# A fused attention and mixture-of-experts kernel: first four tiles prepared in pieces of 1, 1 and 2, side stages of attention in places of their own, local values moved by DMA

## The reference

```
x = layernorm(x + A(x))        # A: two attentions, each with a residual of its own
x = layernorm(x + F(x))        # F: a shared expert and 2 of 8 routed experts

A(x):  x = x + global_attn(rmsnorm(x, w1))     # causal over 1024, keys and values through a latent of 32
       x = x + local_attn(rmsnorm(x, w2))      # causal, window of 32
       both: 16 query heads, 4 key/value heads, 8 features each; rope, then each
       head of q and k divided by its rms; softmax(q k / sqrt(8)) v; output matrix wo
F(x):  shared = (silu(x sg) * (x su)) sd       # width 256
       p = sigmoid(x router + bias); the two largest, divided by their sum, weigh
       the outputs of their experts, each of width 256 like the shared one
```

## Time and profile before

| | us |
|---|---|
| median of 3 runs (lowest, highest) | 748.67 (747.52, 750.77) |
| profiled execution | 749.87 |
| its span, first to last instruction | 748.1 |
| busy PE, PEld, DVE, ACT, POOL | 639.4, 344.4, 505.7, 430.6, 379.6 |
| mean granted TensorE clock | 0.971 of full |
| moved by DMA | 47.23 MB |

### The profile page before, as it was taken

One profiled execution on the slowest core, in us unless ns is written; L12 is line 12 of the kernel. 1 busy time (PEld: TensorE's weight loads), 2 busy tenths in 40 slices (PEclk: granted clock), 3 DMA queues, 4 the chain that ended last, 5 costly groups with the idle time before them and its releaser, 6 DMA issues. The chain is left out here.

```text
span 748.1 us, 12565 instructions
## 1 busy us (share of the span) xinstructions
PE 639.4 (85%) x4147; PEld 344.4 (46%) x4147; DVE 505.7 (68%) x1325; ACT 430.6 (58%) x589; POOL 379.6 (51%) x420
## 2 busy tenths in 40 slices
PE   2378988998999999899999889999987999999950
PEld 1223332343453334454434344445765767666840
DVE  2568774467896458799559858658875658344864
ACT  4367876876566775567776644763442554344433
POOL 5366534554534434442153377751477256777831
PEclk9989998999999999999999999999999999999985
DMA  8235555200000000000000001010004122335251
GB/s 255 83 117 204 203 175 203 73 1 1 1 2 1 1 1 15 0 15 15 15 1 1 1 30 40 30 34 0 1 15 122 52 64 75 101 93 160 82 184 57
DMA packets 38126, 47.23 MB, mean 63 GB/s; under 512 B 8960, under 2 KB 35232, under 8 KB 37408
## 3 DMA queue, kind: packets, MB, share of 16 engines
q1 hardware_dynamic: 26976, 35.10, 15.2%
q0 software_dynamic: 4352, 9.05, 3.5%
q10 hardware_dynamic: 6736, 2.30, 1.2%
HBM read 35.29 MB, written 28.98 MB: 86 GB/s over the span
## 5 line engine op out<-in xcount | busy, mean ns | idle before, releaser
L878 ACT ACTIVATE prob<-ps_s 128x1024 f32<-128x1024 f32 x320 | 309.2, 1024 | 145.8 <-PE ps_s L1249 101.0
L1291 PE MATMUL ps_v<-prob,va 128*32 128x512 f32 x1152 | 155.8, 622 | 4.1 <-POOL prob L768 3.9
L1249 PE MATMUL ps_s<-qs,ks 32*128 32x512 f16 x576 | 102.1, 389 | 19.9 <-ACT prob L878 16.2
L768 POOL TENSOR_SCALAR_AFFINE_SELECT prob<-prob 128x1024 f32<-128x1024 f32 x64 | 70.5, 1120 | 42.8 <-ACT prob L878 42.5
L1033 DVE STREAM_TRANSPOSE sums<-ps_v 128x512 f32<-128x512 f32 x62 | 44.2, 714 | 68.1 <-PE ps_v L1291 35.1
L1529 POOL DMA_INDIRECT y_rows<-y,to_row x72 | 70.2, 975 | 38.7 <-DVE y L1650 21.1
L1249 PEld LDWEIGHTS ps_s<-qs,ks 32*128 32x128 f16 x576 | 25.3, 91 | 127.1 <-ACT prob L878 80.6
L1562 ACT ACTIVATE gated<-ps_gu 128x512 f32<-128x512 f32 x46 | 27.5, 597 | 79.3 <-PE ps_gu L1757 65.7
L1757 PE MATMUL ps_gu<-weights,rows_t 128*128 x144 | 68.2, 596 | 0.5 <-ACT rows_t L1567 0.5
L1285 PE MATMUL ps_v<-prob,vd 128*128 128x256 f32 (+1 forms) x292 | 59.1, 349 | 4.3 <-DVE marked L1053 3.9
L1138 PE MATMUL ps_p<-ident_half,zeros 128*128 128x512 f16 x216 | 52.8, 387 | 7.0 <-DVE k_rows L1024 2.5
(11 more groups left out here) (233 smaller groups left out, 1086.4 us busy)
## 6 DMA issues: line engine op xcount, KB each, us to landing
x_rows<-in_blank SPq DMA_DIRECT2D x8, 2112.0 KB, 8.8
rows<-x_rows SPq DMA_DIRECT2D x72, 66.0 KB, 2.0
chosen_y<-y_rows SPq DMA_DIRECT2D x8, 512.0 KB, 6.7
weights<-in_weights SPq DMA_DIRECT2D x1, 3456.0 KB, 13.7
out<-result ACTq DMA_DIRECT2D x8, 256.0 KB, 2.2
marked<-in_hidden SPq DMA_DIRECT2D x3, 512.0 KB, 5.4
r_in<-in_hidden SPq DMA_DIRECT2D x6, 256.0 KB, 2.7
y_rows<-y,to_row POOLq DMA_INDIRECT x72
```

Of the source, the lines that this page charges most:

```text
L768: pool.affine_select(out=probs_at(n, 0, SLOT_COLS), in_=probs_at(n, 0, SLOT_COLS), compare_op=ALU.is_ge, fill=0.0, base=0, pattern=[[0, SL ...
L878: act.activation(probs_at(n, 0, SLOT_COLS), scores_at(n, 0, SLOT_COLS), ACT.Exp, scale=HD ** -0.5 / GAIN ** 2).then_inc(exped, 1)
L1249: last = pe.matmul(scores_at(n, j * BANK, BANK).rearrange("p (r q) -> p r q", r=REP), ks[b % QUERY_BATCHES][rows, kt * P:(kt + 1) * P], qs ...
L1291: last = pe.matmul(bank[g * VW:(g + 1) * VW, :, :], va[b % VALUE_BATCHES][:, kt, g, :], probs_at(n + g // 2, g % 2 * BANK, BANK).rearrange ...
```

## The change

- `CHUNK_ORDER` begins with three small global chunks, (0,0,0) and (0,0,1) of one tile and (0,0,2) of two (`SMALL`), then (0,0,4) of four, so 18 chunks; chunks are now named by their first tile. All preparation stages work on `size_of(chunk)` tiles. The small ones use the table `PREPARE_SMALL` (11 steps), (0,0,4) `PREPARE_FIRST` (21 steps); local chunks have `PREPARE_LOCAL`.
- The first slot stands at step -29 and the first chunk starts at -40, the next at -37, -32, -27; two steps of pause stand before tile 1 and before tile 4, the pause ahead of the last local tiles has 40 steps instead of 38. By the planner's tables the first slot of tile 4 moves from step 20 to -5, and every later slot by 25 (after the pause 23); chunk (0,1,0) starts at -13 (before 0), the two next 13 and 14 steps earlier, (0,2,0) 16, and from (1,0,4) on all by 23 to 25.
- `turn_values`, `move_values` and the matrices `select` are gone. SP sends the value rows to `vd` itself, 16 transfers of 32 partitions x 4 x 32 bytes for each local chunk.
- Steps have three places: -0.5 (after scores on PE, after band on DVE), -0.25 (after wo, after add), 0 (after weighings, after sums). The tables have places in halves and quarters.
- SP's program follows the steps too.
- The zeroing of `kd` and `vd`, the ones and the band have other steps; the reciprocals of the sums are written into PSUM beside the sums instead of a buffer of their own.
- `WARM` has 155 products at 30 places instead of 221 at 30.
- In `expert_phase` the late tokens, turns, router, choice and `FINAL_SENDS` (8 to 10) come later by one to three pairs, and the last gather by one.

```diff
-FIRST_STARTS = (-37, -16)
-CLEAR_VALUES_AT, CLEAR_BLOCKS_AT = {-33: 1, -32: 2}, {-31: 0, -15: 1}
-ONES_AT, BLOCK_ONES_AT = {-20: 1, -18: 2}, {-6: 0, -4: 1}
-BAND_AT, REPEAT_BAND_AT = -36, -31
+FIRST_STEP = -29
+PAUSES = {(1, 3, 4): 40, (0, 0, 1): 2, (0, 0, 4): 2}
+SMALL = {(0, 0, 0): 1, (0, 0, 1): 1, (0, 0, 2): 2}
+FIRST_STARTS = (-40, -37, -32, -27)
+CLEAR_VALUES_AT = {-38: 1, -37: 2}
+CLEAR_KEYS_AT = {-22: 1, -28: 0}
+CLEAR_BLOCKS_AT = {-31: 0, -23: 1}
+ONES_AT = {-18: 2, -14: 1}
+BLOCK_ONES_AT = {-12: 0, 5: 1}
+BAND_AT = -8
+REPEAT_BAND_AT = -5
+PREPARE_SMALL = [(0, "square"), (1, "sum"), (1, "invert"), (1, "refine"), (2, "scale"), (3, "turn_tokens"), (3, "move_tokens"),
+                 (4, "project", 0), (4, "rotate", 0), (5, "add"), (5, "square_heads"), (6, "sum_heads"), (6, "invert_heads"),
+                 (7, "normalise"), (7, "split_heads"), (8, "pair_parts"), (9, "turn_parts", 2), (9, "move_parts", 2),
+                 (10, "turn_parts", 0), (10, "move_parts", 0)]
+PREPARE_FIRST = [(-0.25, 'square'), (1, 'sum'), (1, 'invert'), ..., (19, 'turn_parts', 2), (18, 'move_parts', 2), ..., (20, 'move_parts', 1)]
+PREPARE_LOCAL = [(0, 'square'), (3.5, 'sum'), ..., (15, 'rotate', 1), (16, 'add'), (16.75, 'send_values'), (16, 'square_heads'), ...]
+PLACES = (-0.5, -0.25, 0)
+START_DELAYS = {(1, 3, 4): 3, (0, 2, 4): 2, (1, 0, 0): -1, (1, 0, 4): 8, (1, 1, 4): -3, (0, 2, 0): -2, (1, 2, 4): -2}
+WARM = {('wo', 2): (3, 0), ('turn_parts', 3, 2): (3, 0), ('weigh', 9): (3, None), ('weigh', 37): (7, 0), ..., ('turn_parts', 2, 2): (9, 0)}
...
         def at_every_step(attend, stages):
             for s in STEPS_ALL:
-                attend(s)
-                for chunk, name, *where in beside.get(s, []):
-                    if name in stages:
-                        stages[name](chunk, chunk_number[chunk], *where)
+                for part, place in zip(attend, PLACES):
+                    part(s)
+                    for chunk, name, *where in beside.get(s + place, []):
+                        if name in stages:
+                            stages[name](chunk, chunk_number[chunk], *where)
...
+            def send_values(chunk, k):
+
+                _, b, c = chunk
+                sp.wait_ge(rope, rope_value(k, 1, "values"))
+                if b < 2:
+                    sp.wait_ge(cleared, GROUPS * (b + 1))
+                if b >= 2:
+                    sp.wait_ge(weighed, batch_weighed(1, b - 2))
+                blocks = vd[b % 2][:, c * P // KEYS:(c + CT) * P // KEYS, :].rearrange("p (t b) m -> p b t m", b=P // KEYS)
+                for of in range(P // KEYS):
+                    for g in range(GROUPS):
+                        sp.dma_start(blocks[g * KEYS:(g + 1) * KEYS, of, :, g * VW:g * VW + HD],
+                                     v_rows[of * KEYS:(of + 1) * KEYS, :, g * HD:(g + 1) * HD]).then_inc(values_out, 16)
...
+                inverse = sums_bank(q)[:, 0, 0:REP * P // VW].rearrange("p (r b) -> p r b", r=REP)
+                dve.reciprocal(inverse, sums[:, :, :, HD]).then_inc(inverses, 1)
...
-            def turn_values(chunk, k):
-
-                for b in range(4):
-                    last = pe.matmul(side_values(chunk)[:, b], select[:, b].rearrange("p g n -> p (g n)"), v_rows[:],
-                                     start=True, stop=True)
...
-LATE_TOKENS = {4: (0, 4), 5: (4, 8)}
-LATE_TURNS = (5, 6)
-LOGITS_AT, LATE_EXP_AT = 7, 9
-FINAL_SENDS = 8
+LATE_TOKENS = {4: (0, 2), 5: (2, 5), 6: (5, 8)}
+LATE_TURNS = (7, 9)
+LOGITS_AT = 10
+LATE_EXP_AT = 10
+FINAL_SENDS = 10
-GATHERED_AT = {0: 34, 1: 36, 3: 38, 2: 40, 6: 45, 4: 46, 7: 47, 5: 48}
+GATHERED_AT = {0: 34, 1: 36, 3: 38, 2: 40, 6: 45, 4: 46, 7: 47, 5: 49}
```

More of the change, by code:

```diff
@@ L4 @@
+import math
 from contextlib import ExitStack
@@ L78 @@
 ROW = D + 4
-SCAN, ENDS = 8, 8
+SCAN = 8
+ENDS = 8
 SHIFTS = tuple(tuple(2 ** n for n in range(6) if 2 ** n < tiles) for tiles in SHARE_TILES)
 END_SHIFTS = tuple(tuple(2 ** n for n in range(6) if 2 ** n < entries) for entries in LISTS)
-ROUTE = [(0, "route_add"), (1, "route_stats"), (2, "route_moments"), (4, "route_power"), (8, "route_token"), (10, "route_turn"), (12, "route_move"), (14, "route_logits"), (15, "route_bias")]
-CHOOSE = [(17, "choose_exp"), (18, "choose", "prob"), (20, "choose", "first"), (22, "choose", "second"),
-          (24, "choose", "third"), (26, "choose_rank"), (26, "choose", "weights"), (28, "choose", "totals"), (30, "choose", "scan"),
-          (32, "choose", "slots"), (34, "choose", "slot1"), (36, "choose", "slot2"), (42, "choose", "blocks"),
-          (46, "choose", "ends"), (50, "choose", "starts"), (54, "choose", "past"), (58, "choose", "rows"),
-          (62, "choose", "experts")]
@@ L95 @@
-ROUTE_AT = {0: 172, 1: 188, 2: 210, 3: 0, 4: 0, 5: 0}
+ROUTE = [(0.75, 'route_add'), (2.0, 'route_next'), (1, 'route_stats'), (2, 'route_moments'), (4, 'route_power'), (7.75, 'route_token'), (10, 'route_turn'), (10, 'route_move'), (15.5, 'route_logits'), (15, 'route_bias')]
+CHOOSE = [(17, 'choose_exp'), (18, 'choose', 'prob'), (20, 'choose', 'first'), (22, 'choose', 'second'), (24, 'choose', 'third'), (26, 'choose_rank'), (26, 'choose', 'weights'), (29, 'choose', 'totals'), (29, 'choose', 'scan'), (32, 'choose', 'slots'), (34, 'choose', 'slot1'), (36, 'choose', 'slot2'), (42, 'choose', 'blocks'), (46, 'choose', 'ends'), (50, 'choose', 'starts'), (54, 'choose', 'past'), (58, 'choose', 'rows'), (62, 'choose', 'experts')]
@@ new lines @@
+SENDS_FROM = 41
+SENT_INSIDE = 7
+SEND = [(SENDS_FROM + i * 3 // 2, "send", i) for i in range(2 * SHARE_TILES[0])]
+SECOND_INSIDE = [(17, 'choose_exp'), (17, 'choose', 'prob'), (18, 'choose', 'first'), (20, 'choose', 'second'), (20, 'choose', 'third'), (25, 'choose', 'weights'), (26, 'choose_rank'), (32, 'choose', 'totals'), (33, 'choose', 'scan'), (34, 'choose', 'slots'), (35, 'choose', 'slot1'), (36, 'choose', 'slot2')]
+INSIDE = [CHOOSE + SEND, SECOND_INSIDE + [(SECOND_INSIDE[-1][0] + 10 + i, "send", i) for i in range(SENT_INSIDE)]]
@@ L303, in slot_order @@
 def slot_order():
-    order, step, local = [], 0, iter((1, b, qt) for b in range(B) for qt in range(TPB))
+    order, step, local = [], FIRST_STEP, iter((1, b, qt) for b in range(B) for qt in range(TPB))
     banks = {}
@@ L405, in stages_beside @@
         for chunk, start in zip(CHUNK_ORDER, starts):
-            for when, *stage in PREPARE:
-                if stage[0] in ("turn_values", "move_values", "spread_keys") and not chunk[0]:
+            for when, *stage in table_of(chunk):
+                if stage[0] in ("send_values", "spread_keys") and not chunk[0]:
                     continue
@@ L426, in banks_of @@
                 moved = (SIDE_MOVES[stage[0]], *(("totals",) if stage[0] == "choose_rank" else stage[1:]))
-                free_from[bank] = start_of[chunk] + moved_at[k][moved] + 1
+                of_table = moved_at[k] if chunk[0] == 2 else {tuple(stage): when for when, *stage in table_of(chunk)}
+                free_from[bank] = start_of[chunk] + of_table[moved] + 1
                 bank_for[chunk, *stage] = bank
@@ L440, in attention_layers @@
     for chunk, start in zip(CHUNK_ORDER, starts):
-        needed = min(slot_step[n] for n, (q, _, _) in enumerate(slots) if tiles[q][:2] == chunk[:2] and tiles[q][2] // CT == chunk[2])
-        assert start + PREPARE_STEPS <= needed, (chunk, start, needed)
+        needed = min(slot_step[n] for n, (q, _, _) in enumerate(slots) if chunk_of[tiles[q]] == chunk)
+        assert start + max(when for when, *_ in table_of(chunk)) < needed, (chunk, start, needed)
     route_starts = []
     for k, (_, b, c) in enumerate(ROUTED):
-        start = max(ROUTE_AT[k], added_step[position[1, b, c * CT + CT - 1]] + 1)
+        start = max(ROUTE_AT[k], added_step[position[1, b, c + CT - 1]] + 1, route_starts[-1] + ROUTE_STEPS if k else 0)
         while banks_of(starts, route_starts + [start]) is None:
@@ L1228, in score @@
                 layer, b, qt = tiles[q]
[L1229 to L1231 removed]
+                chunk = chunk_of[tiles[q]]
+                if qt == chunk[2] and (kt == qt and pair == 0 or kt is None):
+                    pe.wait_ge(parts_out, turns_before(chunk_number[chunk] + 1))
                     if layer:
```

317 lines of the change are left out of this document (166 added, 151 removed).

## The result

The changed kernel takes **703.86 us** (median of 4 runs, 701.55 to 705.95) against 749.57 us for the kernel before in the same comparison: ratio 0.9392, 95% interval 0.9349 to 0.9436, 45.7 us faster. The forecast was 724 us, range 711 to 741: the direction was right, the size was off by 20 us.

A forecast was written before the change was run, and what follows sets the result against it. Neither PE nor ACT alone was taken to bound attention, but queues worked in a written order, with engines waiting for each other. 749.87 - 17.6 + 2 - 5 - 4 = 725.3 profiled, so 724 us; range 711 to 741.

The forecast's parts named there:

- Term C: Attention, 67 to 500 us: half and quarter places let side stages go ahead of a weighing; -4 us, -15 to +10.
- the rival in which side stages hold the queues up: Preparations and routings: stages placed half a step early make queues wait; gain gone or 753 us; chance 0.07.
- the places are worth what the idle time allows: Rival for the waiting in attention: Term C is -15 and Term A -20, so 711 us; chance 0.12.
- the mark: First score of tile 4, the 21st exponential: from 66.6 us before to 49.0 forecast, bounds 43.4 to 57.
- Term A: Start of the kernel: small first chunks bring attention earlier, -17.6 us (-23 to -9.6), with +2 for pushed-back steps.
- Both signs named for a wrong prediction: 21st exponential after 57 us; stretch from there to the last chunk's first weighing not 0 to 20 us shorter.
- Half speed at the start: Rival: PE runs at 1.2 GHz early, the 21st exponential comes at 57 us, kernel 736 us; chance 0.14.
- Term B: Local chunks: values by DMA replace PE's selection products and DVE's copies; -5 us, -10 to 0, transfers cost nothing.
- Term D: Experts at the end: later dispatch with four sends fewer behind it, but later rows; 0 us, -3 to +3.

The follow-up runs named there:

- u_start: The changed kernel with its first eight tiles prepared in two chunks of four and the first slot at step 0, as before; 146 zero products: 721.46 us.
- u_peval: The changed kernel with local values spread by PE's selection products and DVE's copies as before, in place of the transfers: 725.62 us.
- u_whole: The changed kernel with every half and quarter place of the preparation and routing tables rounded up to the whole step: 749.96 us.
- c_more: The changed kernel with ten more products of zeros at the two places after 100 us where its trace shows the lower clock: 705.63 us.

## Why the prediction was wrong

**The direction was right** (faster, at 0.90), and so was the account of what bounds the kernel: queues in a written order, in which engines wait for each other. The size was missed by 20 us.

**Term C is the step that failed.** It took the places for "a half step, less than the 1.5 us of a slot" and bounded them by a tenth and a fifth of the 77 us of waiting: -4, at most -15. (A tenth of 77 is 7.7; the +10 of that passage is neither.) The trace after shows 30.9 of 75.3 us, two fifths, and the runs show 40 to 46 us lost when the places alone go. The terms measured one by one add up to more than the 45.7 us of the whole, so they are not independent: the start and the transfer gain nothing with whole places. What the step missed is that an in-order queue turns half a step into the length of a wait for another engine. The row that said so was quoted, 68.1 us of DVE ahead of L1033, but I used it as evidence for the rival in which side stages hold the queues up. Its other reading was the right one: in the kernel before all of DVE's side stages stood behind that wait already, and the change put some of them ahead of it. The rival "the places are worth what the idle time allows" had this mechanism and 0.12 of the chance, and its 711 us was still too careful, with a start worth 20 us in it that the mark doesn't show (6.0). I argued against it with the 80.6 us that PE's weight loads waited for exponentials; afterwards that row is 85.0, unchanged, while ACT's wait for scores went from 101.0 to 67.3. The row did not bound the gain.

**Term A** had its first exponential right (21, measured 22.07) and its mark wrong (49, measured 60.6): -6.0 us at the mark instead of -17.6. The chunk of tiles 4 to 7 was to rotate at 27.4 us and did at 43.9; from there to its first exponential 16.7 us passed, forecast 16 to 21.2. The failed pieces are the steps from one rotation to the next. The four chunks rotate at 11.3, 16.7, 26.0 and 43.9 us, so 5.4, 9.3 and 18.0 us apart, where 4.2, 4.2 and 5.5 were forecast: the last one makes 12.5 of the 16.5 us by which the rotation is late. The forecast counted the buffer alone, not the token stages in queues that attention now shared. That the start is worth 17.6 us at the end agrees with the term by number, not by reason, and that is luck: what u_start loses behind the mark the term did not have. Both signs named for a wrong prediction came: the 21st exponential after 57 us, and the stretch from it to the last chunk's first weighing 42 us shorter (445.4 for 487) instead of 0 to 20. The range of 711 to 741 was also narrower than the bounds of A and C, which added up give 708 to 746; 703.86 lies outside even those.

**Half speed at the start** (rival): the view of the granted clock gives 1.00 in every stretch from 20 to 60 us, as the forecast asked for. But this trace has its first record of the clock at 34.2 us, and the view shows 1.00 where there is none; and the products say otherwise up to about 33 us, by these rows of the changed kernel:

```profile
29.75 1.94 PE L1345 MATMUL ps_v<-prob,va 128*32 128x512 f32 x8 [0.84 <-POOL prob L833]
31.96 0.61 PE L1303 MATMUL ps_s<-qs,ks 32*128 32x512 f16 x2 [0.28 <-ACT prob L945]
...
38.31 0.39 PE L1303 MATMUL ps_s<-qs,ks 32*128 32x512 f16 x2 [0.79 <-DVE qs L1088]
```

1.94 us for eight weighing products is the 1.93 of 0.50 and not the 1.06 of full speed. So the early start did run at 1.2 GHz for a while. Its products from 20 to 32 us last 6.6 us, which at full speed would be half: at most 3.3 us of the 11.6 by which the mark was late. "TensorE: Matmul & The Clock Gate" of the Trainium skill, Part 1, has the throttled clock as the state from which a kernel starts, and these durations agree with it.

**Term B** was -5, too small: the transfer is worth 13.0 us (8.5 by the ratios) without zeros in the old order and 21.8 in the new. In the trace PE is spared 8.0 us from the 21st to the 301st exponential and I had counted half. Set side by side over that stretch, u_peval has PE busy for 369.1 us against 355.1 and idle for 32.6 against 23.9: the 8.0 of selection products, 6.1 by which the rest last longer (clock 0.96 against 0.99), 8.7 of waits. That the transfers cost nothing held: SP needed 0.64 us for each of 16 rather than 0.43, and PE shows no wait for them.

```profile
483.59 10.24 SPq L696 DMA_DIRECT2D vd<-v_rows  x16
...
506.03 3.72 PE L1339 MATMUL ps_v<-prob,vd 128*128 128x256 f32 x20 [0.24 <-ACT prob L974]
```

The 22.4 us from the first transfer to the first weighing of the last chunk hold them. That weighing was to start at 525 to 533 us and starts at 506.0 (553.85 before).

**Term D** was right: from the last exponential to the end 193.9 us, 194.5 before. The last share's dispatch starts 72.0 us after the last exponential instead of 68.5, 3.5 later for 3.75 forecast. With four sends fewer behind it POOL's last send starts 161.2 us after the last exponential instead of 162.5, 1.4 earlier where 1.3 was forecast, and PE waits 2.74 us for the rows of the last share, where 3.1 was.

```profile
577.87 0.96 POOL L1580 DMA_INDIRECT x_rows<-marked,index  x1 [0.30 <-issue]
...
601.97 0.44 PE L1837 MATMUL ps_x<-ident,rows 128*128 128x128 f32 x2 [2.74 <-DMA rows<-x_rows]
...
666.98 0.96 POOL L1588 DMA_INDIRECT y_rows<-y,to_row  x1 [0.30 <-issue]
```

## What to carry to other kernels

In an in-order queue, look at what stands at its head. If an engine waits long for one thing (here DVE for a tile's weighed sums, 68 us in all), price each small instruction behind that wait by the wait and not by its own length: a sum of squares and 0.6 us of 128x4 arithmetic, put half a step ahead in each of 14 chunks, were worth 22 us, because another engine's queue stood behind their result. Products that only keep the clock up belong to one order of the queue; place them anew when anything in it moves, and judge an edit without them as well.

## What the runs showed of the hardware that was not expected

- The view of the granted clock reads 1.00 at the start of the execution while products last as at 1.2 GHz (1.94 us for eight at 29.75 us). The traces have no record of the clock before 34.2 us (35.4 in the kernel before). Durations of a known product are the better witness there.
- What time at the lower level costs depends on what lies beside it: 3.6 us for 10.2 where zeros took it away in u_whole, and 0 for 3.4 in c_more, each by one trace. In c_more it also came up where nothing was edited, 6.8 us from the 221st to the 261st exponential, a stretch of 57.1 us against 54.8: 2.3 us for 6.8.
- A queued issue of a 4 KB transfer in 32-byte pieces took SP 0.64 us, where an earlier issue of one transfer had taken 0.43. In the same trace the issues of the experts' rows, 66 KB each, follow each other every 0.52 us.
